# Two images' tiles of the experts first: their table, rows and first weights moved into the phase before

## The reference

```python
def _L1_ffn_ref(x, Wr, br, W1, b1, W2, b2):
    xt = x.reshape(-1, d)                       # 4096 tokens, d = 256
    route_prob = softmax(xt @ Wr + br)          # E = 8 experts
    routes = argmax(route_prob, axis=-1)
    def expert_step(acc, inp):                  # H = 1024
        h = gelu(xt @ w1 + bb1, approximate=False)
        y = h @ w2 + bb2
        return acc + y * (routes == e)[:, None], None
    ...
t = t + _L1_ffn_ref(_ln_t(t), ...)
```

## Time and profile before

| | |
|---|---|
| median of 3 runs | 1238.78 us (1238.21 to 1240.36) |
| the profiled execution | 1240.58 us, of which 1238.8 us from its first to its last instruction |
| busy: PE, DVE, POOL, ACT | 91%, 55%, 46%, 35% of the span |
| mean granted TensorE clock | 0.945 of full |
| output phase to expert phase | VectorE's first instruction of the expert phase at 916.56 us |
| TensorE's first of the expert phase | 937.20 us |

### The profile page before, as it was taken

The page is one execution under the profiler, slowest core; times in us unless marked ns, Lnnn a source line. Parts: engine busy times, 40 slices in busy tenths (PEclk is TensorE's granted clock), DMA queues, the critical chain, the costliest instruction groups (busy, mean ns, idle before and its releaser), DMA issues. The chain is left out here.

```text
span 1238.8 us, 23452 instructions
## 1 busy us (share of the span) xinstructions
PE 1124.2 (91%) x7604; PEld 822.3 (66%) x7605; DVE 676.7 (55%) x1491; ACT 434.1 (35%) x511; POOL 570.6 (46%) x565
## 2 busy tenths in 40 slices
PE   6899999896679999999999999998726999999995
PEld 3577878685455555555555555556516999999994
DVE  4264747556467777777777777715742333333331
ACT  1303232320225555555555555564420111111110
POOL 0003030303047777877787878840361444444443
PEclk8799999897689999999999999998857999999998
DMA  6204361323152232323232323134455565565551
GB/s 210 60 1 128 135 188 68 119 87 131 73 167 76 80 94 60 94 60 94 60 94 67 101 68 100 31 121 136 149 118 175 194 215 193 191 203 208 191 193 61
DMA packets 61608, 148.44 MB, mean 120 GB/s; under 512 B 11360, under 2 KB 31776, under 8 KB 59904
## 3 DMA queue, kind: packets, MB, share of 16 engines
q1 hardware_dynamic: 53184, 123.39, 31.1%
q0 software_dynamic: 7536, 22.96, 5.6%
q10 hardware_dynamic: 848, 1.58, 0.5%
HBM read 104.58 MB, written 39.87 MB: 117 GB/s over the span
## 5 line engine op out<-in xcount | busy, mean ns | idle before, releaser
L217 DVE TENSOR_REDUCE s_nmax<-ps_v 128x1 f32<-128x512 f32 x484 | 311.3, 685 | 114.2 <-PE ps_v L211 104.0
L967 POOL TENSOR_TENSOR h_added<-h_added,h_expd 128x1024 f32<-128x1024 f32 x124 | 295.5, 2383 | 37.6 <-ACT h_expd L990 29.7
L990 ACT ACTIVATE h_expd<-ps_v 128x1024 f32<-128x1024 f32 x128 | 131.1, 1025 | 155.5 <-PE ps_v L1016 150.0
L1713 PEld LDWEIGHTS ps_h<-xs_c,lnt 128*128 128x128 f32 x1248 | 147.0, 194 | 4.8 <-issue 2.9
L1713 PE MATMUL ps_h<-xs_c,lnt 128*128 128x128 f32 x1248 | 147.5, 277 | 2.3 <-DVE xs_c L1665 2.3
L1723 PE MATMUL ps_y<-w,vals_t 128*128 x624 | 141.2, 379 | 0.6 <-DVE ys L1678 0.6
L1030 PE MATMUL h_ps_o<-h_expd,s_vh 128*32 128x256 f32 x2048 | 137.8, 387 | 0.0
L424 POOL TENSOR_TENSOR a_res<-a_res,a_lnt 128x2048 f32<-128x2048 f32 x4 | 18.2, 4539 | 253.0 <-DVE a_lnt L123 253.0
L990 ACT ACTIVATE h_expd<-h_ps_e 128x1024 f32<-128x1024 f32 x128 | 130.3, 1018 | 0.0
L1754 ACT ACTIVATE vals_t<-ps_h 128x1024 f32<-128x1024 f32 x39 | 39.9, 1024 | 255.8 <-DVE ps_h L1658 255.8
L1723 PEld LDWEIGHTS ps_y<-w,vals_t 128*128 128x128 f32 x624 | 115.5, 190 | 15.1 <-issue 1.0
(11 more groups left out here) (222 smaller groups left out, 1592.2 us busy)
## 6 DMA issues: line engine op xcount, KB each, us to landing
lnt<-in_w SPq DMA_DIRECT2D x38, 1024.0 KB, 4.9
qk_scr<-a_head_hi SPq DMA_DIRECT2D x16, 512.0 KB, 2.6
qk_scr<-a_head_lo SPq DMA_DIRECT2D x16, 512.0 KB, 3.6
w<-in_w SPq DMA_DIRECT2D x8, 1024.0 KB, 5.9
xs<-xs_scr SPq DMA_DIRECT2D x39, 128.5 KB, 2.1
a_x_t<-in_x_t POOLq DMA_DIRECT2D x4, 1024.0 KB, 9.2
r_scr<-a_res POOLq DMA_DIRECT2D x4, 1024.0 KB, 6.1
v_scr<-res SPq DMA_DIRECT2D x4, 1024.0 KB, 3.8
```

Of the source, the lines that this page charges most:

```text
L217: self.nc.vector.tensor_reduce(self.nmax[k][:, nb, half:half + 1], ps_m[:, half, :], AX.X, ALU.max, negate=True).then_inc(self.v_max, 1)
L967: nc.gpsimd.tensor_tensor(total[:, :], (expd[:, 0, :] if m == 1 else total[:, :]), expd[:, m, :], ALU.add).then_inc(g_add, 1)
L990: nc.scalar.activation(expd[:, m, :], flat(ps_e[m % 2]), ACT.Exp, scale=SCALE).then_inc(a_exp, 1)
L1713: last = nc.tensor.matmul(ps_h[k][:, c // 4, c % 4 * P:(c % 4 + 1) * P], w1_now[k][:, t, c * P:(c + 1) * P], xs_c[:, t, :], start=(t == 0) ...
```

## The change

`READY` = 2 x 8 - 7 = 9 full tiles of 128 rows exist for certain once images 0 and 1 are routed, whatever the split over eight experts. These nine become tiles 0 to 8. A class `Schedule` makes the table in two parts: `early` (27 small VectorE instructions on 9 tiles, in the output phase between `positions(2)` and `router(3)`) and `late` (two parts of 13 on the other 30 tiles, in the expert phase, after VectorE's work on tile 0 and on tile 1). At the end of the output phase SP waits for the rows of images 0 and 1, loads the first layer's weights of tiles 0 and 1, the rows of tile 0, and, when those are there, the rows of tile 1. There are two row buffers `xs`, so a load waits for the tile two earlier. Image 3's scatters move behind GpSimd's `take(1)`, four before and four behind `take(2)`. SP waits for the padding, for images 2 and 3 and for the late table ahead of tile 8. TILES stays 39.

```diff
+READY_IMAGES = 2
+READY = READY_IMAGES * NB - (E - 1)
+SCANNED = 1
...
+        def step(ins):
+            self.n += 1
+            ins.then_inc(self.v_step, 1)
+            dve.wait_ge(self.v_step, self.n)
+        return step
+    def tiles_of(self, dve, out, have, keep, full):
+        n = READY_IMAGES * NB if full else TB
+        over = self.over[:, :, 0:n]
+        step, vec = self.stepped(dve), self.nc.vector
+        step(vec.scalar_tensor_tensor(self.count[:, :], have, float(1 - P) if full else 0.0, keep["region"][:, :], ALU.add, ALU.subtract))
+        step(vec.tensor_tensor(over, self.count[:, :].rearrange("p (e o) -> p e o", o=1).to_broadcast([P, E, n]),
+                               keep["steps128"][:, 0:n].rearrange("p (o t) -> p o t", o=1).to_broadcast([P, E, n]), ALU.is_gt))
+        step(vec.tensor_reduce(out[:, :], over, AX.X, ALU.add))
+    def scan(self, dve, ntile):
+        step, vec, base = self.stepped(dve), self.nc.vector, self.base
+        step(vec.memset(base[0][:, 0:1], 0.0))
+        step(vec.tensor_copy(base[0][:, 1:E], ntile[:, 0:E - 1]))
+        c, shift = 0, 1
+        while shift < E:
+            step(vec.tensor_copy(base[1 - c][:, 0:shift], base[c][:, 0:shift]))
+            step(vec.tensor_tensor(base[1 - c][:, shift:E], base[c][:, shift:E], base[c][:, 0:E - shift], ALU.add))
+            c, shift = 1 - c, 2 * shift
+    def place(self, dve, ntile, rows, keep, first, n):
+        step, vec, base = self.stepped(dve), self.nc.vector, self.base
+        over_e = lambda ap: ap.rearrange("p (t o) -> p t o", o=1).to_broadcast([P, n, E])
+        over_t = lambda ap: ap.rearrange("p (o e) -> p o e", o=1).to_broadcast([P, n, E])
+        tiled, tiled2, end = self.tiled[:, 0:n, :], self.tiled2[:, 0:n, :], self.end
+        texp, start, tile_no = self.texp[:, first:first + n], self.start[:, first:first + n], keep["tile_no"][:, 0:n]
+        c = SCANNED
+        step(vec.tensor_tensor(end[:, :], base[c][:, :], ntile[:, :], ALU.add))
+        step(vec.tensor_tensor(tiled, over_e(tile_no), over_t(end[:, :]), ALU.is_ge))
+        step(vec.tensor_reduce(texp, tiled, AX.X, ALU.add))
+        step(vec.tensor_scalar(texp, texp, float(E - 1), None, ALU.min))
+        vec.tensor_copy(self.texp_i[:, first:first + n], texp).then_inc(self.v_experts, 1)
+        step(vec.tensor_tensor(tiled, over_e(tile_no), over_t(base[c][:, :]), ALU.subtract))
+        step(vec.tensor_scalar(end[:, :], ntile[:, :], -1.0, 0.0, ALU.add, ALU.max))
+        step(vec.tensor_tensor(tiled2, tiled, over_t(end[:, :]), ALU.min))
+        step(vec.scalar_tensor_tensor(tiled, tiled2, float(P), over_t(rows[:, :]), ALU.mult, ALU.add))
+        step(vec.tensor_tensor(tiled2, over_e(texp), over_t(keep["expert_no"][:, :]), ALU.is_equal))
+        step(vec.tensor_tensor(tiled, tiled, tiled2, ALU.mult))
+        step(vec.tensor_reduce(start, tiled, AX.X, ALU.add))
+        vec.tensor_copy(self.start_i[:, first:first + n], start).then_inc(self.v_start, 1)
+    def early(self, dve, keep, have):
+        self.tiles_of(dve, self.full, have, keep, full=True)
+        self.scan(dve, self.full)
+        self.place(dve, self.full, keep["region"], keep, 0, READY)
+        step, vec = self.stepped(dve), self.nc.vector
+        step(vec.tensor_scalar(self.used[:, :], self.base[SCANNED][:, :], -1.0, float(READY), ALU.mult, ALU.add))
+        step(vec.tensor_scalar(self.used[:, :], self.used[:, :], 0.0, None, ALU.max))
+        step(vec.tensor_tensor(self.used[:, :], self.used[:, :], self.full[:, :], ALU.min))
+    def late(self, dve, keep, have, part):
+        if part:
+            self.place(dve, self.ntile, self.rows, keep, READY, TILES - READY)
+            return
+        self.tiles_of(dve, self.ntile, have, keep, full=False)
+        step, vec = self.stepped(dve), self.nc.vector
+        step(vec.tensor_tensor(self.ntile[:, :], self.ntile[:, :], self.used[:, :], ALU.subtract))
+        step(vec.scalar_tensor_tensor(self.rows[:, :], self.used[:, :], float(P), keep["region"][:, :], ALU.mult, ALU.add))
+        self.scan(dve, self.ntile)
...
+def rows_out(pool, io, keep, sems, b, which=range(NB)):
+    done = sems["last_scattered" if b == B - 1 else "ready_scattered" if b < READY_IMAGES else "scattered"]
+    for i in (b * NB + j for j in which):
         pool.indirect_dma_start(io["xs_scr"][:, :], bass.IndirectOffsetOnAxis(ap=keep["pos"][:, i:i + 1], axis=0),
                                 keep["lnt"][:, i, :], None).then_inc(done, 16)
+def first_weights(keep):
+    both = keep["lnt"][:, :, :].rearrange("p t c -> p (t c)")
+    return [both[:, k * CT * H:(k + 1) * CT * H].rearrange("p (t h) -> p t h", h=H) for k in range(2)]
...
+                table = keep["schedule"]
+                sp.wait_ge(sems["ready_scattered"], 16 * READY_IMAGES * NB)
+                sp.wait_ge(table.v_experts, 1)
+                for k, w1 in enumerate(first_weights(keep)):
+                    e = sp.value_load(table.texp_i[0:1, k:k + 1], min_val=0, max_val=E - 1)
+                    sp.dma_start(w1, io["w1"][bass.ds(e, 1)].rearrange("o (t p) m -> p (o t) m", p=P)).then_inc(sems[f"w1_in{k}"], 16)
+                sp.wait_ge(table.v_start, 1)
+                for k in range(2):
+                    row = sp.value_load(table.start_i[0:1, k:k + 1], min_val=0, max_val=E * REGION - P)
+                    if k:
+                        sp.wait_ge(sems["xs_in"], 16)
+                    sp.dma_start(keep["xs"][k][:, :], io["xs_scr"][bass.ds(row, P), :]).then_inc(sems["xs_in"], 16)
                 sp.wait_ge(t_stored, 16 * B)
...
+                    if b == B - 1:
+                        keep["schedule"].early(dve, keep, prior[:, READY_IMAGES * NB, :])
...
+                def load(i, k):
+                    row = sp.value_load(start_i[0:1, bass.ds(i, 1)], min_val=0, max_val=E * REGION - P)
+                    sp.dma_start(xs[k][:, :], io["xs_scr"][bass.ds(row, P), :]).then_inc(xs_in, 16)
+                def weights(i, k):
+                    e = sp.value_load(texp_i[0:1, bass.ds(i, 1)], min_val=0, max_val=E - 1)
+                    sp.wait_ge(pe_hid, i - 1)
+                    sp.dma_start(w1_now[k], io["w1"][bass.ds(e, 1)].rearrange("o (t p) m -> p (o t) m", p=P)).then_inc(w1_in[k], 16)
+                def tokens(i, k):
+                    sp.wait_ge(pe_xs, i - 1)
+                    sp.wait_ge(g_taken, i - 1)
+                    sp.wait_ge(xs_in, 16 * i)
+                    load(i, k)
+                def loads(first, end):
+                    with sp.Fori(first, end) as p:
+                        for k in range(2):
+                            tokens(2 * p + 2 + k, k)
+                            weights(2 * p + 2 + k, k)
                 pad_rows(sp, range(0, E // 2))
...
-                def load(i):
-                    row = sp.value_load(start_i[0:1, bass.ds(i, 1)], min_val=0, max_val=E * REGION - P)
-                    sp.dma_start(xs[:, :], io["xs_scr"][bass.ds(row, P), :]).then_inc(xs_in, 16)
...
-                def tokens(i):
-                    sp.wait_ge(pe_xs, i)
-                    sp.wait_ge(g_taken, i)
-                    load(i)
+                loads(0, EARLY_PAIRS)
                 sp.wait_ge(padded, 16 * E)
+                sp.wait_ge(scattered, 16 * (B - 1 - READY_IMAGES) * NB)
                 sp.wait_ge(last_scattered, 16 * NB)
-                sp.wait_ge(v_start, 1)
-                load(0)
-                sp.wait_ge(v_experts, 1)
-                weights(1, 1, first=True)
-                tokens(1)
-                with sp.Fori(0, (TILES - 3) // 2) as p:
-                    for k in range(2):
-                        tokens(2 * p + 2 + k)
-                        weights(2 * p + 2 + k, k)
-                tokens(TILES - 1)
+                sp.wait_ge(v_start, 2)
+                sp.wait_ge(v_experts, 2)
+                loads(EARLY_PAIRS, PAIRS)
+                tokens(TILES - 1, (TILES - 1) % 2)
                 weights(TILES - 1, 0)
...
-                rows_out(pool, io, keep, sems, B - 1)
...
+                take(0, 0)
                 nc.gpsimd.tensor_copy(id_in[:, :], ids[:, 0:1]).then_inc(g_ids, 1)
                 pool.wait_ge(g_ids, 1)
                 gather()
-                take(1)
-                take(2)
+                take(1, 1)
+                rows_out(pool, io, keep, sems, B - 1, range(0, 4))
+                take(2, 0)
+                rows_out(pool, io, keep, sems, B - 1, range(4, NB))
...
-                tiles(dve, tile)
+                tile(0, first=True)
+                for n in range(2):
+                    schedule.late(dve, keep, prior[:, TB, :], n)
+                    tile(n + 1, parity=1 - n)
+                pairs(dve, tile, 1, EARLY_PAIRS)
+                dve.wait_ge(v_experts, 2)
+                pairs(dve, tile, EARLY_PAIRS, PAIRS)
...
+                for some in ((0, EARLY_PAIRS), (EARLY_PAIRS, PAIRS)):
+                    if some[0]:
```

(44 more changed lines are left out.)

84 lines of the change are left out of this document (30 added, 54 removed).

## The result

The changed kernel takes 1227.72 us, median of 7 runs (1225.68 to 1233.28); the ratio to 7 runs of the kernel before beside it, whose median is 1242.63, is 0.9892 [0.9871, 0.9913]. On 1238.78 us, the time that the forecast started from, that is 1225.4 (1222.8 to 1228.0): faster, by some 13 us instead of the 17.1 forecast.

A forecast was written before the change was run, and what follows sets the result against it. TensorE alone bounds the expert tiles (7.25 us each); the gain lies in the hole ahead. 18.1 us of removed wait less 1.0 in first tiles takes 1240.58 to 1223.5, less 1.8 to the median: 1221.7; range 1217 to 1229.

The forecast's parts named there:

- T: VectorE's first instruction of the expert phase, the zero for times there; forecast at 918.8 us, 2.2 later than before.
- the first turn: TensorE's first expert-phase work, on tile 0: forecast at 919.1 instead of 937.20, a gain of 18.1 us.
- The estimate of 915.1 for the three loads: Output phase: by the skill's DMA formula, three loads on one queue are through after 7.1 us; sum then 1219.5.
- First tiles: Start of expert phase: waits for tile 2's rows and weights, each 0 to some 2 us, together taken as 1.0.
- A: Rival, crowding: early loads meet image 2's scatters, VectorE starts near 924.6, first tiles wait; 1227.5 to 1230.7 us, chance 0.20.
- the 909.8: Output phase: time from which 2.75 MB at 198 GB/s take 13.9 us, putting block end at 923.7.
- B: Rival: output block's end not delayed, no first-tile waits; gain 20.3 us, 1218.5 or 1216.6 us, chance 0.10.
- C: Rival: the hole moves, tile 2's rows or weights so late that PE stands as before; 1238 to 1239, chance 0.05.
- D: Rival, slower: GpSimd's round per tile sets the pace, 37 us per us beyond its 1.0 us reserve; chance 0.05.

The follow-up runs named there:

- e3: Changed kernel with the row loads of tiles 0 and 1 ahead of the two weights in the output phase; 1231.89 us, ratio 0.9924 to the kernel before.
- e5: Changed kernel with SP's early loads of tiles 0 and 1 moved to the start of the expert phase; 1234.82 us, one run.
- the second execution: The changed kernel measured and profiled once more, nothing altered; 1231.02 us, ratio 0.9902 to the kernel before.
- e1: Changed kernel with SP's padding writes behind the loads of tiles 2 and 3, ACT's behind tile 1's gelu; 1228.98 us, ratio 0.9901 to the kernel before.
- e2: Changed kernel with all eight of image 3's scatters behind GpSimd's take of tile 2; 1232.04 us, ratio 0.9931 to the kernel before.
- e11: e10 plus SP waiting for GpSimd's take before issuing weights, so they leave behind the gather; 1222.60 us, ratio 0.9851 to the kernel before.
- e4: Changed kernel with 50 unused TensorE transposes at the end of the output phase; 1232.63 us, ratio 0.9936 to the kernel before.
- e8: Changed kernel with padding writes spread one at a time over tiles 2 to 5, all eight scatters ahead of take(2); 1226.80 us, ratio 0.9868 to before.
- e10: e8 plus early loads ordered weights 0, rows 0, rows 1, weights 1, and e4's transposes; 1223.95 us, ratio 0.9860 to the kernel before.
- e12: e11 with the late table's second part cut in two, behind tiles 1 and 2; 1221.49 us, ratio 0.9847 to the kernel before.

## Where the forecast was right, and the step that failed

**What was right.** `router(3)` at 909.38 (forecast 909.6), the end of `positions(3)` at 914.71 (914.9), weights at 908.09 (908.0), rows of tile 0 issued at 910.44 (910.2) and tile 1's, which wait for them, at 918.36 (rows landed by 917.9 forecast). T is 919.34 (918.8), the first turn 919.49 (919.1): 17.71 of the 18.1 us. The pace of a tile stayed, 7.24 to 7.25 us; TensorE waited for no weights. The estimate of 915.1 for the three loads, from the Trainium skill (DMA: Bandwidth & Descriptors, Anatomy of one DMA), is 3 us too early here: the rows were waited for until some 918, with image 2's scatters on the same engines.

**What ended the block.** SP's drain was to be last, with GpSimd's left at 916.3. GpSimd's ended at 919.08, since the loads hold it up (e3, e5), and was last by 0.2 us; in the second execution SP was last by some 0.4. That the drain was put 2.8 us too early was a mistake, and it is luck that it cost next to nothing: SP's end, rightly placed, lay beside it.

**The step that failed is "First tiles".** 1.0 us was taken, and 4.66 measured. The wait for tile 2's rows itself, 1.48 us, lies within the 0 to 2 that the prediction gave; asked for at T + 13.2 (12.8 forecast), the rows came at T + 14.6, near the far end of T + 8.2 to 15.0. What the term put at nothing is what this wait of TensorE set off: from the rows to the second layer it takes 0.97 us (933.98 to 934.95) where 0.22 is usual, and the second layer goes at 1.2 GHz for most of its length (5.40 for 3.46, 1.94 us). The first layer of tile 0 is 0.50 longer besides. 1.48 + 0.75 + 1.94 + 0.50 = 4.67. With the 17.71 us of the first turn that leaves 13.05, and the two profiled executions are 1240.58 - 1227.72 = 12.86 us apart. In the second execution the wait was 2.23 us, over the 2 that the prediction allowed, and the second layer took 6.75. e1 shows that the rows are late through the padding ahead of their load, with a share of the scatters (e2); it also shows that the bunch then costs as much at another place. The late table, taken as hidden, is hidden in the changed kernel but for 0.2 us (sums 7.55 and 7.14 us apart around it, 7.24 otherwise); when the sum ahead of it is late it holds TensorE up (e1, e3, e11).

**The rivals.** A's half of the waits came, the other didn't: the first tiles lost 4.66 us, a little over A's "up to 4.2", but T is only 0.5 us beyond the forecast, not 5.8. The gain, some 13 us, lies between the forecast's 17.1 and A's 8.1 to 11.3; the 909.8 from which A's block end is counted is not worked out in the prediction. B and C did not come. Nothing was slower, but D's mechanism is there: the reserve of GpSimd's round fell from 1.04 to 0.66 us a tile, through the weights, which the second row buffer lets go sooner, not through the rows. In e4, e5, e8 and e10 it is used up. TensorE is still busy throughout in e10 from 1000 to 1200 us, and the price there was some 3 us in all (e11), not 37 for each us.

**What was left.** e12 has 0.9847 [0.9822, 0.9872] of the kernel before, against 0.9892 [0.9871, 0.9913] after: the best run, though the intervals touch. From T to the last sum it is 6.87 us shorter than after. Whether fewer transposes would let the block end sooner, at the drain, wasn't tried. That tile 0's first layer is 0.50 longer than before isn't the change's doing as far as the runs show: it takes 5.43 us in the second execution of the same kernel, and 5.41 to 6.47 in the other runs that start it at the lower clock.

## What to carry to other kernels

Loading ahead across a phase boundary takes a series of latencies off the path, but the work that stood in that series (here the padding) then runs beside the first tiles: ask which load is queued behind it, and spread it before counting the gain. Price a wait of TensorE with the clock that it may lose and the steps that it uncovers; here they were nearly twice the wait, while in e2 (0.82 us) and e3 (2.50) no clock was lost, so read it from the trace. When a buffer removes a wait, look for what that wait kept apart: here weights from a gather.

## What the runs showed of the hardware

GpSimd's drain at a block's end is no constant: it ends 2.7 us behind the last scatter in the kernel before, 2.6 in e5, 3.4 in e3 and 5.6 in the changed kernel, where the DMA engines move 320 GB/s. That it waits for the scatters' landing is inferred from this, since the trace has no landing for the last of them.

Behind eight padding writes in a bunch, with scatters beside them, the DMA engines are taken up for 1.0 to 1.3 of their time while 79 to 127 GB/s are moved; the steady tiles move 198 at 0.58.

A gather of 128 rows landed 2.8 us after its issue when weights left 3.5 us later, 3.3 when they left 0.9 later, 3.7 to 3.9 where the sums ran behind (e4, e8, e10), and 6.1 beside padding (e1).
